# Mamba state scan: every third product with C on GpSimd, four buffers where there were two, sums two steps behind, the gate read from PSUM

## The reference

```
delta = softplus(x @ dt_proj + dt_b)          # [token, channel]
dA[n] = exp(delta * A[:, n])                  # A = -exp(A_log), n = 0..15
dB[n] = delta * B[:, n] * x                   # B, C come from x_proj
h[n]_t = dA[n]_t * h[n]_(t-1) + dB[n]_t       # recurrence over tokens
y = sum_n h[n] * C[:, n] + D * x
out = (y * silu(z)) @ out_proj
```

## Time and profile before

| | us |
|---|---|
| median of 3 runs | 1271.48 (1271.02 to 1272.04) |
| the profiled execution, its own time | 1269.26 |
| its span (first to last instruction) | 1267.4 |
| mean granted TensorE clock, share of full speed | 0.912 |
| busy in the span: PE / DVE / ACT / POOL | 968.5 / 947.0 / 634.4 / 632.4 |

### The profile page before, as it was taken

How to read it: one execution, slowest core, us unless ns; L and a number is a source line. 1 busy time by engine, 2 the same in 40 slices (tenths; PEclk the granted TensorE clock), 3 DMA queues, 4 the chain that set the end, 5 groups by cost and what they waited for, 6 DMA issues and landing times.

```text
span 1267.4 us, 12569 instructions
## 1 busy us (share of the span) xinstructions
PE 968.5 (76%) x3012; PEld 551.5 (44%) x3012; DVE 947.0 (75%) x1236; ACT 634.4 (50%) x1155; POOL 632.4 (50%) x452
## 2 busy tenths in 40 slices
PE   5307988668878996389999999876767666675896
PEld 2103333223324653278888888532222222223684
DVE  4995787799987647656666666587999999965564
ACT  4424475600026466156555565777455555553455
POOL 3721054746651014167777777502666666613572
PEclk9758999779998998699999999987899999996998
DMA  2000110000002000176666666200000000000661
GB/s 71 0 0 1 53 58 15 1 0 0 1 0 71 1 16 7 37 157 145 144 157 152 142 146 149 60 1 0 1 0 0 0 0 0 1 13 11 152 151 34
DMA packets 18639, 61.62 MB, mean 49 GB/s; under 512 B 2560, under 2 KB 12416, under 8 KB 12800
## 3 DMA queue, kind: packets, MB, share of 16 engines
q1 hardware_dynamic: 18608, 61.26, 20.6%
HBM read 59.54 MB, written 1.70 MB: 48 GB/s over the span
## 4 chain that ended last, share of the span: by engine, by line
PE 45%; DVE 35%; issue 7%; ACT 5%; POOL 4%; DMA 2%; DVEq 1%; SPq 0%; POOLq 0%; ACTq 0%
PE ps L346 44%; DVE g L1352 5%; DVE g L1155 5%; DVE tmp L1155 4%; DVE y L1602 3%; ACT rstd L735 2%; ACT g L735 2%; POOL g L1142 2%; DVE g L1602 2%; DVE parts L1291 2%; DVE parts L1155 2%; DVE resid L1155 2%; DVE g L1559 1%; DMA g<-coef_scratch 1%; POOL sq L1038 1%
## 5 line engine op out<-in xcount | busy, mean ns | idle before, releaser
L346 PE MATMUL ps<-parts 128*128 128x512 f32 x1800 | 450.0, 408 | 32.6 <-DVE parts L1155 9.7
L346 PEld LDWEIGHTS ps<-parts 128*128 128x128 f32 x1800 | 345.4, 195 | 136.5 <-DVE parts L1155 18.0
L735 ACT ACTIVATE g<-ps 128x512 f32<-128x512 f32 (+3 forms) x322 | 189.9, 597 | 327.1 <-PE ps L346 297.2
L1085 POOL TENSOR_TENSOR parts<-g,parts 128x512 fp32r<-128x512 f32 x168 | 217.6, 1295 | 155.5 <-ACT parts L735 151.5
L346 PE MATMUL ps<-g,arena 128*128 128x512 f32 (+1 forms) x304 | 152.5, 644 | 93.0 <-DVE g L1155 42.5
L1142 POOL TENSOR_TENSOR g<-g 128x1024 f32<-128x1024 f32 x64 | 150.2, 2352 | 132.6 <-ACT g L735 130.9
L1155 DVE TENSOR_TENSOR ps<-g,ps 128x512 f32<-128x512 f32 x168 | 116.9, 696 | 112.5 <-PE ps L346 90.7
L735 ACT ACTIVATE parts<-g 128x512 fp32r<-128x512 f32 (+2 forms) x252 | 126.3, 534 | 30.3 <-DVE g L1451 15.9
L346 PEld LDWEIGHTS ps<-g,arena 128*128 128x128 f32 (+1 forms) x304 | 57.4, 201 | 187.6 <-issue 66.7
L1038 POOL TENSOR_TENSOR sq<-resid 128x512 f32<-128x512 f32 x32 | 35.9, 1122 | 199.0 <-DVE resid L1155 184.7
L1155 DVE TENSOR_TENSOR g<-ps,g 128x512 f32<-128x512 f32 x160 | 110.7, 692 | 32.1 <-DMA g<-coef_scratch 14.2
(11 more groups left out here) (168 smaller groups left out, 1107.2 us busy)
## 6 DMA issues: line engine op xcount, KB each, us to landing
g<-coef_scratch SPq DMA_DIRECT2D x80, 512.0 KB, 6.2
g<-in_moe_dram SPq DMA_DIRECT2D x42, 192.0 KB, 4.8
g<-in_rope_dram SPq DMA_DIRECT2D x1, 2048.0 KB, 9.0
arena<-in_weights_dram SPq DMA_DIRECT2D x1, 1348.5 KB, 5.8
sel<-in_selectors_dram SPq DMA_DIRECT2D x1, 1152.0 KB, 7.2
arena<-in_weights_dram SPq DMA_DIRECT2D x1, 1028.5 KB, 4.9
g<-in_x_dram SPq DMA_DIRECT2D x4, 256.0 KB, 3.8
out_dram<-g SPq DMA_DIRECT2D x4, 256.0 KB, 2.5
```

The source lines that it names most:

```text
L346: return nc.tensor.matmul(o, lhsT, rhs, start=start, stop=stop, **kw)
L735: return nc.scalar.activation(o, i, func, **kw)
L1085: pv.tensor_tensor(hid_lo[:, cols(c)], g[:, 6, (c % 2) * N:(c % 2 + 1) * N], hid_hi[:, cols(c)].bitcast(F32), ALU.subtract).then_inc(s["hl ...
```

## The change

- The loops are written out: all 64 steps stand one behind the other, with constants in place of registers.
- Steps with n = 1, 4, 7, 10, 13 of each chunk (`BY_POOL`, 20 of 64) have their product with C on POOL. POOL cannot read PSUM, so ACT copies C's bank to SBUF first (`copy_c`, into `sq`, two buffers). On POOL the product of step s stands behind the inflow of step s+4.
- Four buffers instead of two for the inflow (g rows 10 and 9) and for the product (`tmp` and `rstd`).
- On PE the piece for step s is now `spread_b(s+3)`, `spread_c(s+1)`, `sum_n(s-2)`.
- On ACT the piece for step s is now copy of B for s+1, exponentials for s, saved column of s-2, copy of C for s-2 where that is a step of POOL's.
- ACT no longer copies the sums out. DVE's gate reads banks 0 and 1, for chunks 0 to 2 within the scan of the next chunk (behind scan 3 of it), for chunk 3 at the end. The next chunk's first `sum_n` waits for the gate.

```diff
+STEPS = 16 * CHUNKS
+BY_POOL = [s for s in range(STEPS) if s % 16 % 3 == 1]
...
+        def inflow(step):
+
+            return two_halves(g[:, 10 if step % 4 < 2 else 9, :], step % 2)
+
+        def with_c(step):
+
+            return two_halves(tmp if step % 4 < 2 else rstd, step % 2)
+
+        def c_copy(step):
+
+            k = BY_POOL.index(step) % 2
+            return sq[:, k * N:(k + 1) * N]
+
+        def by_pool(step):
+            return sum(k <= step for k in BY_POOL)
...
+            def spread_b(step):
 
                 at_least(pe, s["bs_ready"], step)
-                mm(ps[:, B_BANK, :], row(n), bc_rows[:, cols(c)]).then_inc(s["bb_bank"], 1)
-
-            def spread_c(n, c, step):
-                at_least(pe, s["hc_ready"], step)
-                mm(ps[:, C_BANK, :], row(n + 16), bc_rows[:, cols(c)]).then_inc(s["cb_bank"], 1)
-
-            def sum_n(nb, step, stop=False):
-                pe.wait_ge(s["hc_ready"], step + 1)
+                mm(ps[:, B_BANK, :], row(step % 16), bc_rows[:, cols(step // 16)]).then_inc(s["bb_bank"], 1)
+
+            def spread_c(step):
+                if step - 1 in BY_POOL:
+                    pe.wait_ge(s["c_copied"], by_pool(step - 1))
+                elif step:
+                    pe.wait_ge(s["hc_ready"], by_dve(step - 1))
+                mm(ps[:, C_BANK, :], row(step % 16 + 16), bc_rows[:, cols(step // 16)]).then_inc(s["cb_bank"], 1)
...
+            def sum_n(step):
+                if step % 16 == 0:
+                    c = step // 16
+                    at_least(pe, s["yg_ready"], c)
+                    for i in range(2):
+                        mm(ps[:, i, :], diag_d[:, i, :], G(i, c), True, False, skip_group_check=True)
+                if step in BY_POOL:
+                    pe.wait_ge(s["hc_pool"], by_pool(step))
+                else:
+                    pe.wait_ge(s["hc_ready"], by_dve(step))
...
+            for step in range(STEPS + 2):
+                if step + 3 < STEPS:
+                    spread_b(step + 3)
+                if step + 1 < STEPS:
+                    spread_c(step + 1)
+                if step >= 2:
+                    sum_n(step - 2)
+            pe.wait_ge(s["yg_ready"], CHUNKS)
...
-            def state_step(c, k, n, saved=None):
-
-                nb = k % 2
-                step = 16 * c + n
+            def copy_b(step):
...
                 act.wait_ge(s["bb_bank"], step + 1)
-                act.wait_ge(s["db_ready"], step + 1)
-                f(g[:, 8, k * N:(k + 1) * N], ps[:, B_BANK, :], ACT.Copy).then_inc(s["bs_ready"], 1)
-                hold(act, s["hs_done"], step + 1)
+                if step >= 4:
+                    act.wait_ge(s["db_ready"], step - 3)
+                f(g[:, 8, step % 4 * N:(step % 4 + 1) * N], ps[:, B_BANK, :], ACT.Copy).then_inc(s["bs_ready"], 1)
+
+            def state_step(step):
+
+                c, n = step // 16, step % 16
+                if step >= 2:
+                    act.wait_ge(s["hs_done"], step - 1)
                 for i in range(2):
-                    f(decays(nb, i), G(4 + i, c), ACT.Exp,
-                      scale=neg_a[:, bass.ds(n + 16 * i, 1)]).then_inc(s["da_ready"], 1)
-                if saved is not None:
-
-                    f(carried[:, :, bass.ds(saved, 1)], states((k + 2) % 4)[:, :, N - 1:N], ACT.Copy)\
-                        .then_inc(s["carry_saved"], 1)
-
...
+                    f(decays(step, i), G(4 + i, c), ACT.Exp,
+                      scale=neg_a[:, n + 16 * i:n + 16 * i + 1]).then_inc(s["da_ready"], 1)
+
+            def save_carry(step):
+
+                n = step % 16
+                act.wait_ge(s["hs_done"], step + 1)
+                f(carried[:, :, n:n + 1], states(step % 4)[:, :, N - 1:N], ACT.Copy).then_inc(s["carry_saved"], 1)
+
+            def copy_c(step):
+                act.wait_ge(s["cb_bank"], step + 1)
+                if by_pool(step) > 2:
+                    act.wait_ge(s["hc_pool"], by_pool(step) - 2)
+                f(c_copy(step), ps[:, C_BANK, :], ACT.Copy).then_inc(s["c_copied"], 1)
+
+            copy_b(0)
+            for step in range(STEPS):
+                if step + 1 < STEPS:
+                    copy_b(step + 1)
+                state_step(step)
+                if step >= 2:
+                    save_carry(step - 2)
+                    if step - 2 in BY_POOL:
+                        copy_c(step - 2)
...
+                    def b_times_du(step):
+                        pool.wait_ge(s["bs_ready"], step + 1)
+                        if step >= 4:
+                            pool.wait_ge(s["hs_done"], step - 3)
+                        pv.tensor_tensor(inflow(step), g[:, 6:8, cols(step // 16)],
+                                         g[:, 8:9, step % 4 * N:(step % 4 + 1) * N].to_broadcast([P, 2, N]),
+                                         ALU.mult).then_inc(s["db_ready"], 1)
+
+                    def states_times_c(step):
+                        pool.wait_ge(s["c_copied"], by_pool(step))
+                        pool.wait_ge(s["hs_done"], step + 1)
+                        if step >= 4:
+                            pool.wait_ge(s["sum_done"], step - 3)
+                        pv.tensor_tensor(with_c(step), states(step % 4),
+                                         c_copy(step).unsqueeze(1).to_broadcast([P, 2, N]),
+                                         ALU.mult).then_inc(s["hc_pool"], 1)
+
+                    for step in range(4):
+                        b_times_du(step)
+                    for step in range(STEPS):
+                        if step + 4 < STEPS:
+                            b_times_du(step + 4)
+                        if step in BY_POOL:
+                            states_times_c(step)
...
+            def scan(step):
+
+                n = step % 16
                 dve.wait_ge(s["da_ready"], 2 * step + 2)
-                dve.wait_ge(s["db_ready"], step + 5)
-                hold(dve, s["carry_saved"], step + 1)
+                dve.wait_ge(s["db_ready"], step + 1)
+                if step >= 4:
+                    dve.wait_ge(s["carry_saved"], step - 3)
+                    if step - 4 in BY_POOL:
+                        dve.wait_ge(s["hc_pool"], by_pool(step - 4))
                 for i in range(2):
-                    at = slice((2 * (k % 2) + i) * N, (2 * (k % 2) + i + 1) * N)
-                    ins = v.tensor_tensor_scan(states(k)[:, i, :], decays(k % 2, i), g[:, 10, at],
-                                               carry[:, bass.ds(n + 16 * i, 1)], ALU.mult, ALU.add)
+                    ins = v.tensor_tensor_scan(states(step % 4)[:, i, :], decays(step, i), inflow(step)[:, i, :],
+                                               carry[:, n + 16 * i:n + 16 * i + 1], ALU.mult, ALU.add)
                 ins.then_inc(s["hs_done"], 1)
 
-            def times_c(k, step):
-
-                nb = k % 2
+            def times_c(step):
+
                 dve.wait_ge(s["cb_bank"], step + 1)
-                dve.wait_ge(s["sum_done"], step + 1)
-                hold(dve, s["hs_done"], step + 3)
-                tt(tmp[:, 2 * nb * N:(2 * nb + 2) * N].rearrange("p (i n) -> p i n", i=2), states(k),
-                   ps[:, C_BANK:C_BANK + 1, :].to_broadcast([P, 2, N])).then_inc(s["hc_ready"], 1)
-
-
...
+                dve.wait_ge(s["hs_done"], step + 1)
+                if step >= 4:
+                    dve.wait_ge(s["sum_done"], step - 3)
+                tt(with_c(step), states(step % 4), ps[:, C_BANK:C_BANK + 1, :].to_broadcast([P, 2, N]))\
+                    .then_inc(s["hc_ready"], 1)
+
+            def gate(c):
+
+                dve.wait_ge(s["sum_done"], 16 * c + 16)
+                tt(g[:, 2:4, cols(c)], ps[:, 0:2, :], g[:, 2:4, cols(c)]).then_inc(s["yg_ready"], 1)
+
+            scan(0)
+            for step in range(STEPS):
+                if step + 1 < STEPS:
+                    scan(step + 1)
+                if step % 16 == 2 and step > 2:
+                    gate(step // 16 - 1)
+                if step not in BY_POOL:
+                    times_c(step)
+            gate(CHUNKS - 1)
```

More of the change, by code:

```diff
@@ L269, in states, with decays, two_halves, by_dve @@
             return home[:, 2 * (k % 2) * N:2 * (k % 2 + 1) * N].rearrange("p (i n) -> p i n", i=2)
-        def decays(nb, i):
-            return ps[:, DA_BANKS[nb] + i, :]
+        def decays(step, i):
+            return ps[:, DA_BANKS[step % 2] + i, :]
+        def two_halves(home, k):
+            return home[:, 2 * k * N:2 * (k + 1) * N].rearrange("p (i n) -> p i n", i=2)
+        def inflow(step):
[7 more added lines that the diff above has]
+            return sum(k <= step for k in BY_POOL)
+        def by_dve(step):
+            return step + 1 - by_pool(step)
         block = ctx.enter_context(nc.Block())
@@ L671, in sum_n @@
+            def sum_n(step):
[8 more added lines that the diff above has]
+                    pe.wait_ge(s["hc_ready"], by_dve(step))
```

(49 more changed lines are left out.)

11 lines of the change are left out of this document (3 added, 8 removed).

## The result

The changed kernel is slower: 1339.13 us (median of 4 runs, 1337.06 to 1342.45) against 1271.25 us for the kernel before on the same chip (4 runs, 1270.94 to 1272.04). The ratio is 1.0534, with a 95% interval of 1.0515 to 1.0553. The forecast was 1326, with a range of 1300 to 1356. The profiled execution took 1338.01 us, with a span of 1336.2 and a mean granted clock of 0.883 where it was 0.912.

A forecast was written before the change was run, and what follows sets the result against it. DVE was taken to bound the kernel at 3.48 us a step. The new PE and ACT order adds 35.0 us and a slower clock 19.6, on 1269.26: 1323.9, plus 2.2 to the median: 1326, range 1300 to 1356.

The forecast's parts named there:

- What bounds the kernel before: DVE sets the pace at 3.48 us a step: 2.37 from scan to product, 1.11 for the product.
- The ring: Wait chain twice through PE and twice through ACT in each three-step round: 12.65 us against 10.44 before.
- POOL's share: POOL gets 64 + 20 = 84 instructions at 2.34 us, 196 us: fits, product on time by 0.3 us.
- The start: First product at 885.42; exponentials of step 6 at about 903, two or three us either way.
- The rounds: Exponentials of step 6 to step 60: 17 rounds of 12.65 us, three with a fourth step (3.48 more), 225.5 us.
- The clock term: PE's idle stretches of about 2.7 us lower its clock: 1.15 us a round, 19.6 us together; bounds 0 and 3.7.
- The end: After step 60's exponentials: product 62 at 1142.9, late sums until 1151.2, then gate, output matmuls at about 1152.7.
- The sum: Chain loss 35.0 us at full speed plus 19.6 for the clock, 54.6 on 1269.26: 1323.9, as a median 1326.
- The signs named beforehand: Trace signs: three steps in 12.6-14.5 us, DVE idle 3-4 us a round, PE clock 0.85-0.95, output matmuls 7-8 us after product.
- full clock (1307): Rival: the same chain through PE and ACT with no loss of clock, 1307 us; chance 0.20.
- Both bursts slow in every round: Rival: both PE bursts of each round slow, 62.9 us in place of 19.6, 1369 us; chance 0.10.
- The gain: Rival: DVE stays the bound, stage of 203.8 us, -25 us, 1247 us; chance 0.05.

The follow-up runs named there:

- the kernel with the old orders: Changed kernel's straight-line code, four buffers and gate from PSUM, but all products on DVE and the earlier PE and ACT orders: 1267.43 us, ratio 0.9973.
- the kernel with fillers: Changed kernel plus six PE passes of zero weights in nearly every step, adding 0 to bank 0: 1314.86 us, ratio 1.0347.
- the kernel without POOL's products: Changed kernel with all 64 products on DVE, 1321.31 us; with four zero-weight passes added in each step, 1304.49 us.

## Why the prediction was right, step by step

The mechanism was right. The sum came out 14 us short on the profiled execution, mostly by two of its terms: the clock, taken at 19.6 us where it was about 31, and the chunk openings, taken at nothing where they were about 6.

- **What bounds the kernel before.** DVE at 3.48 us a step. Right: the kernel with the old orders has the same pace, and nearly the same time.
- **The ring.** Worked out as 12.65 us for three steps. Right, and to 0.03 us: 12.62 with the clock held up. Each of its two sites was shown by moving one call: spread of B earlier (1246), copy of C earlier (1307).
- **POOL's share.** Costed at its inflow's duration, and on time by 0.3 us. Right: 2.35 us, and 0.34 us ahead of the sum in the round shown. One scan in the whole stage waits for it, for 0.4 us.
- **The start.** I put the exponentials of step 6 at 903; they start at 899.14, 3.9 us earlier. Of these, 2.5 are the first scans (878.12 against 880.65). In the kernel before, ACT's first copy of B waited for an increment of `db_ready` that POOL gave only after it had waited for du: it starts at 877.23, behind 0.96 us for POOL. In the changed kernel that wait is gone, and the copy starts at 874.34. I had not counted this as part of the change. The other 1.4 us are the rough estimate of the first steps.
- **The rounds.** From step 6 to step 60 the copies of C for POOL's steps 4 and 58 lie 1162.50 - 900.46 = 262.0 us apart. Predicted were 225.5, and 19.6 for the clock. In the kernel with fillers the same stretch is 233.0, of which 1.7 are the fall of the clock in one opening round. So at full clock it would be 231.3: 5.8 us over the prediction, nearly all of it chunk openings (opening matmuls 1.3 us and gate 0.6 us, three times), a term that I had at nothing. The other 30.7 us are the clock, by difference, 1.8 us a round where I took 1.15.
- **The clock term.** Of the 17 rounds not one is as short as 12.65; the shortest is 13.74. I had priced a round at one slow burst like that of the earlier trace rows, 0.91 us, and a little more. In the 11 rounds of three steps that hold no opening, every one has a slow burst (2.5 to 3.8 us in place of 1.95) behind ACT's copy of C, and six of them have a second one, behind DVE's product. A slow burst costs 1.2 us in the mean, not 0.91, and these rounds take 14.8 us. So the count and the price were both too low. My argument for a small count, that a slow burst keeps PE busier and so protects the next, holds for five rounds of the eleven; what decides which, no run here shows. The bounds of 0 and 3.7 us held.
- **The end.** Predicted 24.2 us from the exponentials of step 60 to the output matmuls, measured 1186.91 - 1161.18 = 25.7, of which a slow burst explains most.
- **The sum.** -3.9 at the start, +16.9 in the rounds, +1.5 at the end, -0.4 behind the stage: +14.1, from 1323.9 to the profiled 1338.0. The early start hid part of the miss in the rounds; that is luck. (In the ring's sum, the handover to the scan, 1.29 + 0.06, was written as 1.34; it changes nothing.)

The signs named beforehand came out in kind and mostly not in size. DVE waits for ACT's exponentials, ACT's copies of B for PE, and DVE hardly ever for POOL, as said. But the rounds of three steps take 13.7 to 17.0 us where 12.6 to 14.5 was said, the clock in the stage is 0.82 and not 0.85 to 0.95, and the output matmuls start 8.2 us behind the last product, not 7 to 8.

The rivals: full clock (1307) falls with the trace's 0.82. The kernel with its clock held up takes 1315; the 8 us between are the openings and the fillers at the end, less the early start. Both bursts slow in every round (1369; it is the second rival of the list, though the text before it calls it the third) was too much: the time lies between it and full clock. The gain (1247) was 0.05 likely for the change as it stands, and is what it turns into once its condition is met.

## What to carry to other kernels

When work is moved off the bound engine, write out for one round what each of the other engines has in a row, and follow one wait from instruction to instruction until it comes back to where it began. If the ring's sum is over the bound engine's own work, the sum is the new pace, whatever the busy shares say. More buffers help only the resource that they belong to: here the ring runs through two PSUM banks of one buffer each, and the four buffers of the inflow and the product did nothing for it. A change of order did, without one buffer more. A prefetch that is asked for one step earlier by its reader must be issued one step earlier by its writer too.

## What the runs showed of the hardware

- Work that computes nothing can pay. Six passes of zero weights in nearly every step took the granted clock from about 0.8 to between 0.97 and 1.00 in the stage and the time from 1339 to 1315 us, and 17 us came back in the kernel without POOL's products.
- The clock can fall behind short waits. In the changed kernel all eleven bursts behind ACT's copy of C that are named above ran slow, as the one at 978.77 did behind 2.49 us in which PE idled: 3.03 us from spread to spread, where 1.95 is the full pace. The stage ran at 0.82.
- POOL can run nearly full (47.3 of 50 us) beside a DVE that is busy for all 50 us, with 128x1024 products at 2.35 to 2.36 us and scans at 1.26 us. The kernel before has 2.35 and 1.27 us, with POOL busy for 18.8 of 28 us. Here each DVE instruction in the stretch has one input in PSUM.
